# Expert units of 128 rows in place of 256, with the first-layer weights of all experts held on chip

## The chip, the cores and the metric

The kernel runs on one core of a Trainium2 chip. The core has five engines that run side by side and meet at semaphores: TensorE (PE in the rows, with its weight loads as PEld) multiplies, VectorE (DVE) and ScalarE (ACT) work element by element, GpSimd (POOL) issues the indirect DMAs here, and SyncE (SP) issues plain DMAs. Each engine has a sequencer that reads its instructions in order; it executes register loads, waits and branches itself (a q behind the engine's name in the rows) and hands the others to the engine. The metric is the time of one execution on the device in microseconds (us).

## The reference

Two blocks with a residual each: a two-layer graph convolution (mean over neighbours) over 3125 nodes of 256 features and 50,000 edges, and a mixture of 8 experts, of which each node uses 2. Cut to what matters here:

```python
def _moe(tokens, router_w, w1, b1, w2, b2):      # tokens: layernorm(x), 3125 x 256
    probs = softmax(tokens @ router_w.T)          # 8 experts
    rw, re = top_k(probs, 2);  rw = rw / rw.sum(-1, keepdims=True)
    combine = zeros((N, E)).at[arange(N)[:, None], re].set(rw)
    out = tokens
    for e in range(E):
        h = gelu(tokens @ w1[e] + b1[e], approximate=False)
        y = h @ w2[e] + b2[e]
        out = out + combine[:, e:e + 1] * y
    return out
x = x + gnn(layernorm(x), edges, ...)
x = x + _moe(layernorm(x)[None], ...)[0]
```

The 3125 nodes make 6250 pairs of node and expert. On the reference's inputs the experts 0 to 7 get 568, 1013, 238, 1264, 432, 590, 862 and 1283 of them (worked out from the inputs with the reference's router); of the first 1536 nodes come 276, 483, 131, 621, 193, 306, 410 and 652.

## The kernel before

Up to about 454 us TensorE computes the graph convolutions: dense adjacency tiles in SBUF (`adj`, 25 blocks of source nodes) are multiplied with the projected rows, tile by tile of 128 nodes. During the second pass (305 to 454 us) the output of each tile is normed and its two experts are chosen on DVE, and POOL writes each node's row with its routing data (`XW` = 264 numbers: 256 features, two coefficients, two experts, the node's number) to its place in the DRAM table `xs_dram`, which has a region for each expert. From tile 8 on, the part of `adj` that is no longer read takes the second-layer weights and biases of all experts (`ew2_sb`, `eb2_sb`), loaded by SP one expert for each tile.

At the end of the router, each expert's region is padded by `PAIR` rows of zeros (`pad_experts`, 4 DMAs on SP and 4 on ACT), and DVE works out tables with an entry for each unit (L1078 to L1111): its first row (`tab_ri`), its expert (`tab_ei`) and how many units must have landed before its scatter may go out (`tab_wi`). The semaphore `table` tells the others that they are ready. `NTAB` entries (36) stand in each table.

Then comes the expert stage. A unit is `PAIR` = 256 rows of one expert in two halves `h`; the loops run over rounds of `UNITS` = 4 units, here 7 rounds for 28 units. For unit i, buffers go by s = i % 2, the result and id buffers by u = i % 4. Each engine has a fixed order for each unit, written out by hand:

- SP waits until rows of unit i+1 are transposed (`xe_tr`) and their routing data kept (`meta_in`), loads the rows of unit i+3 into `xe` (L470), waits for the hidden layer of unit i (`hid`) and loads the first-layer weights of unit i+2 into `w1_of` (L475). `row_of` (L467) and L474 first load a register from a table.
- PE: `result(i)`, the second layer (L1409; half, then two contraction steps); `hidden(i + 2)`, the first layer (L1398, 4 matmuls with 256 columns, each in two passes); `turn_rows(i + 3)`, 4 transposes (L1389).
- ACT: `weigh(i)`, the sum times the coefficient, one ACTIVATE for each half (L1597); `gelu(i + 2)` (L1588); the copy of the transposed rows (L1582).
- DVE: `result(i)`: loads the expert's number into a register (L1128), waits for `meta_in` and for the landing of the scatter that used the buffer before (`ye_out`), copies the node numbers to `ids` (L1132), waits for `ye_ps`, adds the second-layer bias into `ysum` (L1135). `keep_meta(i + 3)`: waits for the rows, copies the node numbers (L1119), and by a test of the chosen expert sets the coefficient (L1121), once for each half.
- POOL: loads the unit's entry of `tab_wi` into a register (L609), waits for the scatters before it (L612), waits for `ye_in`, and adds the half's 128 rows to `out` in DRAM by an indirect DMA (L616), once for each half.

The order of the work around the change is set by these programs and by the semaphores between them; no scheduler moves anything. A matmul in float32 stands as two instructions, and the profile's count of them is double that of the code.

Of the kernel before, what the change touches and what calls it, by code (L numbers as in the profile page):

```python
# [14 lines left out]
P = 128  # L15
# [4 lines left out]
def build(nc, x, src, dst, w1l, w1r, b1, w2l, w2r, b2, router_w, ew1, eb1, ew2, eb2, out):  # L20
# [41 lines left out]
    PAIR = 2 * P  # L62
# [13 lines left out]
    with ExitStack() as ctx:  # L76
# [174 lines left out]
        assert 2 * NE <= NT and KD == 2  # L251
# [18 lines left out]
        def halves(a):  # L270
            return a.rearrange("p (h n) -> p h n", h=2)

        xe = [halves(expert([2 * XW], F32)) for _ in range(2)]
# [3 lines left out]
        ysum = [halves(expert([2 * D], F32)) for _ in range(2)]  # L277
        ye = [halves(expert([2 * D], F32)) for _ in range(UNITS)]
        xt_ps = [counts_ps[:, s, :] for s in range(2)]
        hid_ps = [counts_ps[:, 2 + s, :] for s in range(2)]  # L280
        y_ps = [halves(bank[2 + s][:, :]) for s in range(2)]
        ids = [expert([2], U32) for _ in range(UNITS)]
        match = [[expert([TOPK], F32) for _ in range(2)] for _ in range(2)]
        tab_c = expert([2 * NTAB], F32)
        tab_id = expert([2 * NTAB], F32)
# [29 lines left out]
                 "ysum_in", "rdeg_in"]  # L315
# [13 lines left out]
        xe_in = [sem(f"xe_in{s}") for s in range(2)]  # L329
        w1_in = [sem(f"w1_in{s}") for s in range(2)]  # L330
# [28 lines left out]
        def pad_experts(engine, of):  # L359

            engine.wait_ge(S["ends"], 1)
            engine.wait_ge(S["zeros"], 1)
            for e in of:
                end = engine.value_load(end_i[0:1, e:e + 1], min_val=e * REGION, max_val=e * REGION + N)
                engine.dma_start(xs_dram[bass.ds(end, PAIR), :].rearrange("(h p) n -> p h n", p=P),
                                 pad_t.rearrange("p (h n) -> p h n", h=1).to_broadcast((P, 2, XW))
                                 ).then_inc(S["padded"], 16)

        @block.sync
        def _(sp):  # L370
# [73 lines left out]
            with sp.Fori(0, NE) as e:  # L444
# [5 lines left out]
                             ).then_inc(S["ew_in"], 16)  # L450
                sp.dma_start(ew(eb2_sb, e, 0), eb2[bass.ds(e, 1), :].to_broadcast((P, D))).then_inc(S["ew_in"], 16)
# [10 lines left out]
            for u in range(UNITS):  # L462
                sp.wait_ge(ye_out[u], 32)
# [5 lines left out]
            def load_rows(row, s):  # L469
                sp.dma_start(xe[s], xs_dram[bass.ds(row, PAIR), :].rearrange("(h p) n -> p h n", p=P)  # L470
                             ).then_inc(xe_in[s], 16)

            def load_w1(i, s):
                e = sp.value_load(tab_ei[0:1, bass.ds(i, 1)], min_val=0, max_val=NE - 1)  # L474
                sp.dma_start(w1_of[s], ew1[bass.ds(e, 1), :, :].rearrange("a (k p) n -> p (a k) n", p=P)  # L475
                             ).then_inc(w1_in[s], 16)
# [6 lines left out]
            load_w1(0, 0)  # L483
            load_rows(row_of(1), 1)
            load_w1(1, 1)
            third_row = row_of(2)
            sp.wait_ge(S["xe_tr"], 1)
            sp.wait_ge(S["meta_in"], 1)
            load_rows(third_row, 0)
            rounds = sp.value_load(nround_i[0:1, 0:1], min_val=MIN_ROUNDS, max_val=MAX_ROUNDS)  # L490

            with sp.Fori(0, rounds) as n:
                for u in range(UNITS):
                    i, s = n * UNITS + u, u % 2
                    row = row_of(i + 3)
                    sp.wait_ge(S["xe_tr"], n * UNITS + (u + 2))
                    sp.sem_inc(S["held"], 1)
                    sp.wait_ge(S["meta_in"], n * UNITS + (u + 2))
                    sp.sem_inc(S["held"], 1)
                    load_rows(row, 1 - s)  # L500
                    sp.wait_ge(S["hid"], n * UNITS + (u + 1))
                    sp.sem_inc(S["held"], 1)
                    load_w1(i + 2, s)

            for u in range(UNITS):
                sp.wait_ge(ye_out[u], rounds * 32 + 32)
# [1129 lines left out]
```

## Time and profile before

| | us |
|---|---|
| median of 3 runs (623.62 to 624.03) | 623.7 |
| span of the profiled execution (its own time in the profile) | 621.3 |
| TensorE busy | 557.1 |
| DVE busy | 351.8 |
| ACT busy | 223.1 |
| POOL busy | 182.1 |
| first load of an expert's rows | 478.19 |
| first and last bias add on DVE (27 steps) | 493.19, 605.21 |
| end of the last scatter-add on POOL | 613.78 |

The profile is of one execution; the span runs from its first to its last instruction, and the run's time holds what lies around it, 2.4 us between the span and the median. Busy shares count the work of an engine and not its register, branch and semaphore instructions. Times on the rows are counted from the start of the span.

### The profile page before, as it was taken

The page shows a single profiled execution, that of the slowest core. Times are in us where ns is not written, and L with a number is a line of the kernel's source. Part 1 is how long each engine was busy: PE and PEld are TensorE (multiplying, and loading weights), DVE is VectorE, ACT ScalarE, POOL GpSimd, SP SyncE. Part 2 cuts the span into 40 slices and gives each one's busy share as a digit, 9 for nine tenths or more (in the row PEclk, how much of TensorE's full clock was granted, in tenths as well). Part 3 has the DMA queues.
Part 4 walks back from the last instruction along what each step waited for, and adds up shares of the span by engine and source line. Part 5 has one row for each costly group of instructions (what it writes and reads, how often), then busy time and mean ns, then how long its engine had stood idle before and what let it go on. Part 6 is the DMA issues. An engine that isn't in the chain of part 4 may idle for free.

```text
span 621.3 us, 11268 instructions
## 1 busy us (share of the span) xinstructions
PE 557.1 (90%) x3021; PEld 331.3 (53%) x3022; DVE 351.8 (57%) x1200; ACT 223.1 (36%) x422; POOL 182.1 (29%) x181
## 2 busy tenths in 40 slices
PE   5999989999999999999999999999930999999991
PEld 3444545555555555554454544544510788887870
DVE  5987656676677667652457576676676133323320
ACT  5666834444444444341001000000000355555551
POOL 4840000000000000000310533534362076667784
PEclk9999999999999999999999999999965799999997
DMA  8421201111110111114621346533326499889992
GB/s 263 134 72 51 89 16 51 52 43 35 52 51 29 50 52 43 34 52 103 205 77 61 121 154 185 170 115 121 97 98 206 133 182 192 165 180 186 178 185 30
DMA packets 70327, 67.01 MB, mean 108 GB/s; under 512 B 11633, under 2 KB 68318, under 8 KB 70286
## 3 DMA queue, kind: packets, MB, share of 16 engines
q1 hardware_dynamic: 53406, 50.61, 27.4%
q0 software_dynamic: 11200, 14.40, 12.2%
q10 hardware_dynamic: 5680, 1.49, 1.1%
q8 instruction: 21, 0.34, 0.2%
q14 instruction: 20, 0.16, 0.1%
HBM read 38.11 MB, written 29.30 MB: 109 GB/s over the span
## 4 chain that ended last, share of the span: by engine, by line
PE 58%; issue 13%; DVE 10%; DMA 7%; POOL 6%; SPq 3%; ACT 1%; POOLq 0%; DVEq 0%; ACTq 0%
PE bank L1256 21%; PE counts_ps L643 6%; PE bank L1246 6%; PE bank L1171 6%; PE counts_ps L1398 6%; DMA adj<-in_L_ffn_w 4%; PE counts_ps L1256 4%; POOL xs_dram L577 3%; PE bank L1409 3%; POOL stat L570 2%; PE counts_ps L1389 2%; DMA y<-y_dram 1%; SPq L474 1%; PE bank L1239 1%; PE bank L1161 1%
## 5 line engine op out<-in xcount | busy, mean ns | idle before, releaser
L1256 PE MATMUL bank<-y,adj 128*128 128x512 f16 x625 | 154.7, 379 | 0.4 <-ACT zt L1464 0.4
L1256 PE MATMUL counts_ps<-y,adj 128*128 128x512 f16 x625 | 144.5, 379 | 1.9 <-DMA y<-y_dram 1.9
L616 POOL DMA_INDIRECT out<-adj x56 | 86.9, 1551 | 52.5 <-ACT adj L1597 27.4
L650 ACT ACTIVATE adj<-counts_ps 128x1000 f32 (+1 forms) x80 | 80.2, 1005 | 61.1 <-PE counts_ps L643 61.1
L1256 PEld LDWEIGHTS counts_ps<-y,adj 128*128 128x128 f16 x625 | 60.6, 101 | 64.7 <-DMA y<-y_dram 3.8
L1256 PEld LDWEIGHTS bank<-y,adj 128*128 128x128 f16 x625 | 57.9, 97 | 59.5 <-issue 13.7
L553 POOL IOTA onehots<- 128x8 int32 x1 | 0.1, 143 | 231.9 <-PE counts_ps L643 231.9
L1398 PE MATMUL counts_ps<-adj 128*128 128x256 f32 x240 | 60.3, 395 | 3.9 <-DMA adj<-in_L_ffn_w 3.6
L1561 ACT ACTIVATE rows<-bank 128x256 f32<-128x256 f32 x25 | 9.6, 383 | 130.3 <-PE bank L1330 119.1
L643 PEld LDWEIGHTS counts_ps<-onehots 125*128 125x128 f16 x640 | 41.0, 98 | 27.1 <-ACT adj L650 10.9
L629 DVE TENSOR_TENSOR onehots<-iota,lo_t 125x1024 f16<-125x1024 f16 x80 | 54.7, 683 | 0.2
L1398 PEld LDWEIGHTS counts_ps<-adj 128*128 128x128 f32 x240 | 45.6, 196 | 15.5 <-issue 8.7
L629 DVE TENSOR_TENSOR onehots<-iota,key_t 125x1000 f16<-125x1000 f16 x80 | 53.8, 673 | 0.0
L643 PE MATMUL counts_ps<-onehots 125*128 125x125 f16 x640 | 51.0, 221 | 2.5 <-DVE onehots L629 2.5
L1409 PE MATMUL bank<-adj 128*128 x224 | 53.0, 379 | 0.0
L1171 PE MATMUL bank<-w,rows 128*128 128x512 f32 x100 | 48.8, 611 | 2.7 <-ACT rows L1449 2.2
L1246 PE MATMUL bank<-w,rows 128*128 128x512 f32 x100 | 47.0, 592 | 0.0
L1135 DVE TENSOR_TENSOR adj<-bank,adj 128x512 f32<-128x512 f32 x28 | 19.4, 692 | 45.2 <-PE bank L1409 41.8
L1597 ACT ACTIVATE adj<-adj 128x256 f32<-128x256 f32 x56 | 25.4, 501 | 49.9 <-DVE adj L1135 41.3
L1409 PEld LDWEIGHTS bank<-adj 128*128 128x128 f32 x224 | 40.5, 190 | 4.4
L1389 PE MATMUL counts_ps<-ident,adj 128*128 128x128 f32 x124 | 20.1, 288 | 16.4 <-DMA adj<-xs_dram 16.4
L909 DVE SCALAR_TENSOR_TENSOR rows<-bank,rdeg,rows 128x256 f32<-128x256 f32 x25 | 12.1, 484 | 39.8 <-PE bank L1256 39.8
(233 smaller groups left out, 621.9 us busy)
## 6 DMA issues: line engine op xcount, KB each, us to landing
adj<-in_L_ffn_w SPq DMA_DIRECT2D x38, 256.0 KB
adj<-xs_dram SPq DMA_DIRECT2D x31, 264.0 KB
rows<-z_dram SPq DMA_DIRECT2D x49, 128.0 KB
z_dram<-zt SPq DMA_DIRECT2D x36, 128.0 KB, 1.7
rows<-in_x SPq DMA_DIRECT2D x24, 128.0 KB
out<-yo SPq DMA_DIRECT2D x24, 128.0 KB
y_dram<-yo SPq DMA_DIRECT2D x23, 128.0 KB, 1.7
y<-y_dram SPq DMA_DIRECT2D x4, 640.0 KB, 6.6
```

The source lines that it names most:

```text
L616: g.indirect_dma_start(out, bass.IndirectOffsetOnAxis(ap=ids[u][:, h:h + 1], axis=0), ye[u][:, h, :], None, bounds_check=N - 1, oob_is_err ...
L629: last = nc.vector.tensor_tensor(oh[0:RUN, slot, :].rearrange("p (g k w) -> p g k w", k=n, w=HALF), iota_4[0:RUN, 0:n, :].rearrange("p (g ...
L643: last = nc.tensor.matmul(counts_ps[:, 2 * slot + bank_of, at * P:at * P + KEYS], stat_g[:, :, h:h + 1].rearrange("p k a -> p (k a)"), mov ...
L650: nc.scalar.activation(adj[:, :, bass.ds(at, GW * WD)].rearrange("p b (h d) -> p b h d", d=WD), counts_ps[:, 2 * (group % 2):2 * (group % ...
L1135: v.tensor_tensor(ysum[s], y_ps[s], ew(eb2_sb, e, 0).rearrange("p (h n) -> p h n", h=1) .to_broadcast((P, 2, D)), ALU.add).then_inc(S["ysu ...
L1171: last = te.matmul(out_of[t % 2][:, :], nrm_t_of[t % 2][:, k * P:(k + 1) * P], w[:, k, :], start=(k == 0), stop=(k == KD - 1))
L1246: last = te.matmul(bank[1][:, :], nrm_t[:, k * P:(k + 1) * P], w[:, k, :], start=(k == 0), stop=(k == KD - 1))
L1256: last = te.matmul(to, adj[:, b, t * P:(t + 1) * P], y[:, b, :], start=(b == 0), stop=(b == NT - 1))
L1389: last = te.transpose(xt_ps[s][:, k * PAIR + h * P:k * PAIR + (h + 1) * P], xe[s][:, h, k * P:(k + 1) * P], ident[:, :])
L1398: last = te.matmul(hid_ps[s][:, m * PAIR:(m + 1) * PAIR], w1_of[s][:, k, m * P:(m + 1) * P], xe_t[s][:, k * PAIR:(k + 1) * PAIR], start=(k ...
L1409: last = te.matmul(y_ps[s][:, h, :], ge_t[s][:, m * PAIR + h * P:m * PAIR + (h + 1) * P], ew(ew2_sb, e, m), start=(m == 0), stop=(m == KD ...
L1597: a.activation(ye[u][:, h, :], ysum[s][:, h, :], ACT.Copy, scale=tab_c[:, bass.ds(i * 2 + h, 1)]).then_inc(S["ye_in"], 1)
```

## The change

`PAIR` becomes 128, so a unit is one block of 128 rows, and there are 52 units in 13 rounds. The halves go, and with them one of the two scatter-adds, weighings, tests and half of the transposes, second-layer matmuls and row loads of a unit; the hidden layer keeps its four matmuls, each with 128 columns. `xe` and `xe_in` get four buffers in place of two, so that the rows of unit i+4 are asked for when those of unit i are transposed. The first-layer weights of all experts are loaded in the second pass with the second-layer ones into `ew1_sb`, the next 8 blocks of `adj`; in the expert stage DVE copies them to `w1_of` (`keep_w1`), where it needs the expert's number in a register. The work on `tab_w` moves behind the flag `table`, with a flag of its own (`before_in`) for POOL. `NTAB` becomes 60.

```diff
-    PAIR = 2 * P
+    PAIR = P
...
+        ew1_sb = adj[:, 2 * NE:3 * NE, 0:2 * KD * D].bitcast(F32)
...
-        xe = [halves(expert([2 * XW], F32)) for _ in range(2)]
+        xe = [expert([XW], F32) for _ in range(UNITS)]
...
             with sp.Fori(0, NE) as e:
...
+                sp.dma_start(ew1_sb[:, bass.ds(e, 1), :].rearrange("p a (k n) -> p (a k) n", n=D),
+                             ew1[bass.ds(e, 1), :, :].rearrange("a (k p) n -> p (a k) n", p=P)
+                             ).then_inc(S["ew_in"], 16)
...
             load_rows(first_row, 0)
-            load_w1(0, 0)
-            load_rows(row_of(1), 1)
-            load_w1(1, 1)
...
+            for u in range(1, UNITS):
+                load_rows(row_of(u), u)
...
                 for u in range(UNITS):
-                    i, s = n * UNITS + u, u % 2
-                    row = row_of(i + 3)
-                    sp.wait_ge(S["xe_tr"], n * UNITS + (u + 2))
+                    row = row_of(n * UNITS + (u + UNITS))
+                    sp.wait_ge(S["xe_tr"], n * UNITS + (u + 1))
...
-                    load_rows(row, 1 - s)
-                    sp.wait_ge(S["hid"], n * UNITS + (u + 1))
-                    sp.sem_inc(S["held"], 1)
-                    load_w1(i + 2, s)
+                    load_rows(row, u)
...
             pool.wait_ge(S["table"], 1)
+            pool.wait_ge(S["before_in"], 1)
...
-                    for h in range(2):
-                        pool.wait_ge(S["ye_in"], n * (2 * UNITS) + (2 * u + h + 5))
...
+                    pool.wait_ge(S["ye_in"], n * UNITS + (u + 3))
...
-            link(v.tensor_tensor(landed, past, over(weight, 2 * NE), ALU.mult))
...
-            dve.wait_ge(S["ew_in"], 16 * 2 * NE)
+            dve.wait_ge(S["ew_in"], 16 * 3 * NE)
...
+            def keep_meta(i, u, arrived):
+                dve.wait_ge(xe_in[u], arrived)
+                v.tensor_copy(tab_id[:, bass.ds(i, 1)], xe[u][:, NODE_ID:NODE_ID + 1])
+                v.scalar_tensor_tensor(match[u], xe[u][:, CHOSEN:NODE_ID], tab_ef[:, bass.ds(i, 1)],
+                                       xe[u][:, COEF:CHOSEN], ALU.is_equal, ALU.mult,
+                                       accum_out=tab_c[:, bass.ds(i, 1)]).then_inc(S["meta_in"], 1)
+
+            def keep_w1(i, s):
+                e = dve.value_load(tab_ei[0:1, bass.ds(i, 1)], min_val=0, max_val=NE - 1)
+                v.tensor_copy(w1_of[s].rearrange("p k n -> p (k n)"),
+                              ew1_sb[:, bass.ds(e, 1), :].rearrange("p a n -> p (a n)")).then_inc(S["w1_in"], 1)
...
+            keep_w1(0, 0)
+            keep_w1(1, 1)
+            link(v.tensor_tensor(landed, past, over(weight, 2 * NE), ALU.mult))
+            link(v.tensor_reduce(tab_w, landed.rearrange("p e j -> p j e"), AX.X, ALU.add))
+            v.tensor_copy(tab_wi, tab_w).then_inc(S["before_in"], 1)
             keep_meta(0, 0, 16)
             keep_meta(1, 1, 16)
-            keep_meta(2, 0, 32)
+            dve.wait_ge(S["hid"], 1)
+            keep_w1(2, 0)
+            keep_meta(2, 2, 16)
+            keep_meta(3, 3, 16)
             with dve.Fori(0, rounds) as n:
                 for u in range(UNITS):
                     result(n * UNITS + u, n, u)
-                    keep_meta(n * UNITS + (u + 3), 1 - u % 2, n * 32 + 16 * ((u + 3) // 2 + 1))
+                    keep_w1(n * UNITS + (u + 3), 1 - u % 2)
+                    keep_meta(n * UNITS + (u + UNITS), u, n * 16 + 32)
...
-                pe.wait_ge(w1_in[s], arrived)
+            def hidden(i, s):
+                pe.wait_ge(S["w1_in"], i + 1)
...
-                    hidden(i + 2, s, n * 32 + 16 * (u // 2 + 2))
-                    turn_rows(1 - s, n * 32 + 16 * ((u + 3) // 2 + 1))
+                    hidden(i + 2, s)
+                    turn_rows(u, n * 16 + 32)
...
-                    turn_rows(i + 3, 1 - s)
+                    turn_rows(i + UNITS, s)
```

What stands on DVE in one unit of the loop before, from the bias add of a unit to the waits ahead of the next unit's copy of the ids (ISA are register steps, some of which wait; TENSOR_LOAD is the load of a register from `tab_ei`):

```order
L1135 TENSOR_TENSOR adj<-bank,adj 128x512
L1118 REGISTER_ALU
L1119 ISA [waits xe_in0]
L1119 COPY adj<-adj 128x2
L1121 ISA
L1121 SCALAR_TENSOR_TENSOR adj<-adj 128x2
L1121 ISA
L1121 SCALAR_TENSOR_TENSOR adj<-adj 128x2
L1128 ISA
L1128 TENSOR_LOAD adj
L1128 ISA x2
L1132 ISA [waits meta_in,ye_out2]
```

The same place on DVE after, from the bias add to the second register load:

```order
L1117 TENSOR_TENSOR adj<-bank,adj 128x256
L1104 ISA
L1104 TENSOR_LOAD adj
L1104 ISA x2
L1105 ISA
L1105 COPY adj<-adj 128x512
L1098 ISA [waits xe_in1]
L1098 COPY adj<-adj 128x1
L1099 ISA
L1099 SCALAR_TENSOR_TENSOR adj<-adj 128x2
L1110 ISA
L1110 TENSOR_LOAD adj
```

and on DVE from there to the next bias add, where before a REGISTER_ALU (L1133) stood ahead of the last wait:

```order
L1110 ISA x2
L1111 REGISTER_ALU
L1114 ISA [waits meta_in,ye_out2]
L1114 COPY adj<-adj 128x1
L1117 ISA [waits ye_ps,ye_in]
L1117 TENSOR_TENSOR adj<-bank,adj 128x256
```

A test has gone, and a second register load with its three register steps, one more step and the copy of 512 numbers have come in between the bias add and the routing data.

SP's loop for one unit before, the load of the weights and that of the rows:

```order
L474 ISA [waits hid]
L474 TENSOR_LOAD adj
L474 ISA x2
L475 ISA
L475 DMA adj<-in_L_ffn_w 128x2x256
L467 ISA
L467 TENSOR_LOAD adj
L467 ISA x2
L496 REGISTER_ALU
L470 ISA [waits xe_tr,meta_in]
L470 DMA adj<-xs_dram 128x2x264
```

and on SP after:

```order
L465 ISA
L465 TENSOR_LOAD adj
L465 ISA x2
L482 REGISTER_ALU
L468 ISA [waits xe_tr,meta_in]
L468 DMA adj<-xs_dram 128x264
```

The weight load and its register load have gone from SP's loop, and the row load no longer stands behind the wait for `hid`.

## Rows read from the trace of the kernel before

**Rows 1.** The page: busy us (share of the span) xinstructions; chain by line; POOL's scatter-adds.

```profile
PE 557.1 (90%) x3021; PEld 331.3 (53%) x3022; DVE 351.8 (57%) x1200; ACT 223.1 (36%) x422; POOL 182.1 (29%) x181
...
PE bank L1256 21%; PE counts_ps L643 6%; PE bank L1246 6%; PE bank L1171 6%; PE counts_ps L1398 6%; DMA adj<-in_L_ffn_w 4%; PE counts_ps L1256 4%; POOL xs_dram L577 3%; PE bank L1409 3%; POOL stat L570 2%; PE counts_ps L1389 2%; DMA y<-y_dram 1%; SPq L474 1%; PE bank L1239 1%; PE bank L1161 1%
...
L616 POOL DMA_INDIRECT out<-adj x56 | 86.9, 1551 | 52.5 <-ACT adj L1597 27.4
```

**Rows 2.** Timeline, one unit: start us, us, engine, line, operation, tiles, count [idle before].

```profile
508.95 1.89 PE L1398 MATMUL counts_ps<-adj 128*128 128x256 f32 x8
...
510.68 0.60 PE L1389 MATMUL counts_ps<-ident,adj 128*128 128x128 f32 x4
...
511.12 1.89 PE L1409 MATMUL bank<-adj 128*128 x8
```

**Rows 3.** Timeline, start of the expert stage.

```profile
478.19 0.41 SPq L470 DMA_DIRECT2D adj<-xs_dram  x1
479.36 0.41 SPq L475 DMA_DIRECT2D adj<-in_L_ffn_w  x1
...
481.73 1.11 PE L1389 MATMUL counts_ps<-ident,adj 128*128 128x128 f32 x4 [15.49 <-DMA adj<-xs_dram]
...
484.70 3.62 PE L1398 MATMUL counts_ps<-adj 128*128 128x256 f32 x8
...
491.06 1.89 PE L1409 MATMUL bank<-adj 128*128 x8
...
493.19 0.69 DVE L1135 TENSOR_TENSOR adj<-bank,adj 128x512 f32<-128x512 f32 x1 [5.49 <-PE bank L1409]
```

**Rows 4.** Timeline, the last bias add.

```profile
605.21 0.69 DVE L1135 TENSOR_TENSOR adj<-bank,adj 128x512 f32<-128x512 f32 x1 [2.59 <-PE bank L1409]
```

**Rows 5.** Timeline of POOL: behind a stall, and the last.

```profile
526.85 1.55 POOL L616 DMA_INDIRECT out<-adj  x1 [3.85 <-issue]
...
612.23 1.55 POOL L616 DMA_INDIRECT out<-adj  x1 [0.30 <-issue]
```

**Rows 6.** Timeline of DVE: bias add to ids, and ids to bias add, without waits.

```profile
529.82 0.69 DVE L1135 TENSOR_TENSOR adj<-bank,adj 128x512 f32<-128x512 f32 x1 [1.95 <-PE bank L1409]
...
531.46 0.17 DVE L1132 CAST adj<-adj 128x2 uint32 x1 [0.60 <-DVE adj L1121]
...
571.48 0.18 DVE L1132 CAST adj<-adj 128x2 uint32 x1 [2.85 <-DMA out<-adj]
571.79 0.69 DVE L1135 TENSOR_TENSOR adj<-bank,adj 128x512 f32<-128x512 f32 x1
```

**Rows 7.** By source line, DVE's sequencer: ns min/median/max, first and last start; then one unit.

```profile
L1128 DVEq TENSOR_LOAD <-adj x28: 301/317/581, 486.4 to 601.5; - x28
...
L1121 DVEq FUSED_REGOPS  x56: 65/82/117, 493.4 to 605.7; - x56
...
L1128 DVEq FUSED_REGOPS  x2: 65/128/190, 530.5 to 530.9; - x2
...
L1131 DVEq EVENT_SEMAPHORE  x1: 50/50/50, 531.2 to 531.2; - x1
```

**Rows 8.** Timeline of DVE across the end of the loop.

```profile
505.24 0.69 DVE L1135 TENSOR_TENSOR adj<-bank,adj 128x512 f32<-128x512 f32 x1 [2.42 <-PE bank L1409]
...
507.50 0.18 DVE L1132 CAST adj<-adj 128x2 uint32 x1 [1.22 <-issue]
```

**Rows 9.** Groups of DVE by form: busy us, mean ns of one.

```profile
L766 DVE CAST adj<-adj 100x500 f32<-100x500 int32 x1 | 0.4, 414 | 0.0
```

**Rows 10.** Windows: us, busy PE, PEld, DVE, ACT, POOL, PEclk, DMA share, GB/s.

```profile
375.00:400.00 25.00, 24.04 (x128) 12.54 (x127) 17.23 (x78) 1.77 (x5) 10.36 (x13) 1.00 0.54 168
...
75.00:85.00 10.00, 7.55 (x53) 4.08 (x52) 6.97 (x13) 3.41 (x5) 0.00 (x0) 1.00 0.27 85
```

**Rows 11.** Timeline: a scatter-add, and a DVE copy that starts beside it.

```profile
509.33 1.55 POOL L616 DMA_INDIRECT out<-adj  x1 [0.30 <-issue]
...
509.96 0.40 DVE L1119 COPY adj<-adj 128x2 f32 x1
```

More of the change, by code:

```diff
@@ L276, in build @@
         ge_t = [expert([KD * PAIR], F32) for _ in range(2)]
[L277 to L285, printed above, removed]
+        ysum = [expert([D], F32) for _ in range(2)]
+        ye = [expert([D], F32) for _ in range(UNITS)]
+        xt_ps = [counts_ps[:, s, 0:KD * PAIR] for s in range(2)]
+        hid_ps = [counts_ps[:, 2 + s, 0:KD * PAIR] for s in range(2)]
+        y_ps = [bank[2 + s][:, 0:D] for s in range(2)]
+        ids = [expert([1], U32) for _ in range(UNITS)]
+        match = [expert([TOPK], F32) for _ in range(UNITS)]
+        tab_c = expert([NTAB], F32)
+        tab_id = expert([NTAB], F32)
         cnt = expert([NE], F32)
@@ L328, in build @@
         scattered = [sem(f"scattered{q}") for q in range(2)]
-        xe_in = [sem(f"xe_in{s}") for s in range(2)]
-        w1_in = [sem(f"w1_in{s}") for s in range(2)]
+        xe_in = [sem(f"xe_in{u}") for u in range(UNITS)]
         ye_out = [sem(f"ye_out{u}") for u in range(UNITS)]
@@ L1382, in _, with turn_rows @@
             prefix(NB - 1)
-            def turn_rows(s, arrived):
-                pe.wait_ge(xe_in[s], arrived)
-                for h in range(2):
-                    for k in range(KD):
-                        last = te.transpose(xt_ps[s][:, k * PAIR + h * P:k * PAIR + (h + 1) * P],
-                                            xe[s][:, h, k * P:(k + 1) * P], ident[:, :])
+            def turn_rows(u, arrived):
+                pe.wait_ge(xe_in[u], arrived)
+                for k in range(KD):
+                    last = te.transpose(xt_ps[u % 2][:, k * P:(k + 1) * P], xe[u][:, k * P:(k + 1) * P], ident[:, :])
                 last.then_inc(S["xe_tr"], 1)
-            def hidden(i, s, arrived):
-                pe.wait_ge(w1_in[s], arrived)
+            def hidden(i, s):
+                pe.wait_ge(S["w1_in"], i + 1)
                 pe.wait_ge(S["xe_t_in"], i + 1)
@@ L1406, in result @@
                 pe.wait_ge(S["ysum_in"], i + 1)
-                for h in range(2):
-                    for m in range(KD):
-                        last = te.matmul(y_ps[s][:, h, :], ge_t[s][:, m * PAIR + h * P:m * PAIR + (h + 1) * P],
-                                         ew(ew2_sb, e, m), start=(m == 0), stop=(m == KD - 1))
+                for m in range(KD):
+                    last = te.matmul(y_ps[s], ge_t[s][:, m * PAIR:(m + 1) * PAIR],
+                                     ew(ew2_sb, e, m), start=(m == 0), stop=(m == KD - 1))
                 last.then_inc(S["ye_ps"], 1)
@@ L1416, in _ @@
             turn_rows(1, 16)
[L1417 to L1420 removed]
+            hidden(0, 0)
+            turn_rows(2, 16)
+            hidden(1, 1)
+            turn_rows(3, 16)
+            pe.wait_ge(S["ew_in"], 16 * 3 * NE)
             pe.sem_inc(S["ysum_in"], 2)
```

79 lines of the change are left out of this document (24 added, 55 removed).

## The prediction

> **What bounds the kernel now.** I read first the table of busy shares, then the stage after 478 us, where the diff works. The busy table alone says TensorE [rows 1]; the views of the expert stage say something finer. The timeline of one unit of 256 rows shows TensorE's pattern, each group's start against the next: 1.73 us of hidden layer, 0.44 of transposes, and a second layer as long as the hidden one, 3.9 us with no hole [rows 2]. The 28 units take 27 steps from the first bias add on DVE at 493.19 to the last at 605.21, so 4.15 a unit: 0.25 more than TensorE needs, and the chain puts 4% of the span (25 us) on the load of the first-layer weights [rows 1, 3, 4]. Behind TensorE stands POOL: 56 scatter-adds of 1.55 us with 0.30 between, 1.86 each, 104 us in 118; most of the rest are three stalls, one of them 3.85, where it has to wait until an earlier expert's rows have landed [rows 1, 5]. At the end POOL alone is late: the last bias add ends at 605.90, the last scatter-add at 613.78, and 7.5 us later the span ends [rows 4, 5]. DVE looks idle. But a busy share counts no register work, and this is what I look at next.
>
> **DVE's sequence, which the busy share hides.** In a unit that waits for nothing, the bias add starts at 529.82 and the copy of the ids, the next step of the loop, at 531.46: 1.64 us [rows 6]. The instructions between them are the copy and the two tests of the routing data and a load of the expert's number into a register: the register rows run from 530.5 to 531.2, so the load costs about 0.74 us with its address and check, though the load itself has a median of 0.317 [rows 7]. From the ids to the next bias add, with nothing to wait for, it takes 0.31 (571.48 to 571.79) [rows 6]. So DVE needs 1.95 a unit of 256 rows, and once in four units 0.6 more for the loop's end (2.26 in place of 1.64) [rows 6, 8]. That is half of 4.15 and costs nothing now.
>
> **Units.** The experts get 568, 1013, 238, 1264, 432, 590, 862 and 1283 rows. Rounded up to 256 that is 28 units in 7 rounds, as the 56 scatter-adds bear out; rounded up to 128 it is 52 units in 13 rounds, with none idle. Work by the row falls by 7%; work by the unit grows by 52/28.
>
> **TensorE after.** Second layer: 4 pairs of load and matmul where 8 took 1.73, 0.87. Transposes: two, 0.22. Hidden layer: still 8 pairs, with 128 columns each. If columns set the time it is 0.87; if the weight load did, more. The nearest row, four transposes of 128 columns in 0.44, has the same shape at 0.11 a pair [rows 2]: the load hides, 0.88. Sum 2.0, with seams 2.05.
>
> **POOL after.** 52 x 1.86 is 97 us. Only one unit (the sixteenth) must wait for the one right before it, three for the second before. At a step above 2 us these stalls fit into POOL's slack, taken as nothing; their upper end is the 4 us of one old stall.
>
> **DVE after, the term that decides.** A unit of half the rows keeps every step of the loop but one test, and gains the copy of the weights with a register load of its own. From 1.95: one test less, 0.2 (its register step of 0.082 [rows 7] and the dispatch); one register step less before the bias add, 0.1; a second register load, 0.74; the issue of the weight copy, 0.16 (a register step as that of a test, 0.082, and a dispatch [rows 7]); a quarter of the loop's end, 0.15. Sum 2.70 a unit. The work of the copy itself (0.42, as a cast of 500 elements took 0.414 [rows 9]) lies behind the next register load and costs nothing on top; without that cover it would be 0.42 x 52, 22 us. Bounds: 2.55 when all steps are at their shortest, 2.85 when the loads average 0.37 (their longest is 0.581). I take 2.70: only the count of steps is new, each step's price is a row. DVE is then later than TensorE (2.05) and POOL (1.86), and everyone waits for it: TensorE for the copied weights and the free result bank, ACT for the sum, POOL for the weighed rows.
>
> The Trainium skill, page "DMA: Bandwidth & Descriptors", section "Latency and other measured facts", gives a register load a floor of about 600 ns; the rows here have a median of 317, so the measurement decides, and by the page two loads would make the step 3.26.
>
> **What is taken away and moved ahead of the loop.** The 28 loads of 256 KB leave SP's queue, and the row loads follow each other one step of SP apart instead of two, 1.17 [rows 3]. The eight weight loads now go out on SP in tiles 8 to 15 of the second pass, at most 1.17 of SP time each, ahead of the next tile's rows; TensorE is busy 24.04 of 25 us there [rows 10] and two tiles ahead of DVE's need, so nothing, at most 1 us. The padding writes halve and the sum of 16 x 36 moves behind the flag "table", but the tables grow from 36 to 60 columns: the flag comes 0.7 earlier. First rows are asked for at 477.0 instead of 478.19.
>
> **The start.** Before: load at 478.19, transposes at 481.73, hidden layer of unit 0 at 484.70 in 3.4 us at half clock, second layer of unit 0 at 491.06, bias add at 493.19 [rows 3]. After: load of unit 1 at 478.2, so its transposes can start at 481.7 as unit 0's did; from 481.8 the first hidden layer and second one take half, 1.7 each, and two more transposes 0.43 each: 483.5, 483.9, 485.6, 486.05; second layer 1.7 at half clock, 487.8; bias add at 488.0. DVE's own work ahead of the loop (two copies, the moved sum, 3 us) is done by 486. Clock: that first hidden layer takes 3.62 where one in the loop takes 1.89 [rows 2, 3], half clock; at 75 to 85 us the granted clock is 1.00 (2.4 GHz) with TensorE busy 7.55 of 10 [rows 10]. A step of 2.7 with 2.0 of work is about that share, so full clock after the start; nothing added.
>
> **The sum.** Last bias add: 488.0 + 51 x 2.70 = 625.7. From there 0.42 of add (an estimate: 0.69 for 512 columns, half of it and a fixed part), 0.17 to ACT, 0.51 + 0.08 to POOL, 1.55 of scatter-add, 7.5 to the end: 10.25. Span 635.9, 14.6 over 621.3. The median is 2.4 over the profiled span, added on both sides: **638.3**. By terms: the start gains 5.2, the end 5.8 (one scatter-add is queued at the end instead of several), the steps cost 25.7 (137.7 for 112.0). The forecast's own range is 626 (2.55, start at 486.5) to 649 (2.85, start at 490).
>
> **Rivals.**
> A. *DVE is not late* (chance 0.09): if register work overlaps more than the rows say, TensorE's 2.05 is the step: 488.0 + 104.6 + 10.25 + 2.4 = 605. For it: DVE has 57% busy and TensorE 90% in the page; the weight loads on the path are gone. Against it: the 1.64 and 0.31 were measured with no wait in them. The side turns at (621.3 - 10.25 - 488.0) / 51 = 2.41 us a unit: the second register load must cost under 0.45.
> B. *POOL becomes the bound* (0.08): copies of DVE and the descriptor work of POOL stand in each other's way. In the trace a DVE copy of two elements takes 0.40, where the copies of the ids take 0.17 and 0.18 [rows 6], when it starts 0.63 after a scatter-add of POOL: and ends when the scatter-add is 1.03 old [rows 11]. A copy of 0.42 in each unit would make POOL's step 1.86 + 0.42 = 2.28: 489.2 + 51 x 2.28 + 1.55 + 7.5 + 2.4 = 617. It decides only if DVE's own step is under 2.28, so if A's condition holds. Under my forecast it costs nothing.
> The rule is that of the Trainium skill, page "SBUF", section "SBUF: two separate sides": an fp32 copy within SBUF locks GpSimd out while it writes descriptors; the row agrees that one waits for the other, here DVE for POOL.
> C. *Register loads slow down* (0.03): at the 0.6 of the longest row, 2 x 0.28 more a unit, 3.26: 667.
> D. *DVE's engine waits for POOL's port in nearly every unit* (0.04): its 1.46 of work (0.17, 0.42, 0.42, 0.16, 0.29) and a whole scatter-add of 1.55 in series give 3.0: 654. Against it: the copy of [rows 11] came through 1.03 after the scatter-add's start, not at its end.
> E. *No change* (0.02): a step near 2.41.
>
> That the change does something else is hardly possible: the loads, copies and 13 rounds follow from the code and the counts; three rows over 1280 in the last expert make its eleventh unit, but 51 units are 13 rounds too.
>
> **How the numbers follow.** Forecast 0.74, A 0.09, B 0.08, C 0.03, D 0.04, E 0.02. The time is the forecast's, 638.3. Slower by over 0.2% (1.2 us, about what a measurement of this kernel can tell from no change): 0.74 + 0.03 + 0.04 = 0.81; within 0.2%: 0.02; faster: 0.17. For 8 in 10 the range takes in B and the forecast: 616 to 651.
>
> **What would show it.** Right: bias adds on DVE 2.6 to 2.8 apart with almost no idle time put down to TensorE, scatter-adds over 2.5 apart, TensorE's busy share of the stage near 75%, the first bias add near 488. Wrong: bias adds 2.1 to 2.3 apart (A or B; in B with gaps of POOL at 0.30 and scatter-adds of 2 us), scatter-adds unchanged but DVE copies of 1 us and more (D), a granted clock of 0.50 beyond 490 us, or a second pass whose last full tile on TensorE ends after 455.

## The result, and the profile after

The changed kernel takes 639.19 us (median; 638.79 to 639.73), the kernel before 623.66 in the same comparison: a ratio of 1.025, 95% interval 1.0236 to 1.0263. It is 2.5% slower. The forecast was 638.3, in a range of 616 to 651.

Of the page of the changed kernel: busy us (share of the span) xinstructions; the first steps of the chain by engine and by line; the scatter-adds.

```profile
PE 563.7 (88%) x3185; PEld 329.4 (52%) x3186; DVE 383.0 (60%) x1316; ACT 233.6 (37%) x491; POOL 174.3 (27%) x173
...
PE 46%; issue 16%; DVE 16%; DVEq 11%; POOL 5%; DMA 3%; ACT 1%; POOLq 0%; SPq 0%; ACTq 0%
PE bank L1246 21%; PE counts_ps L625 6%; PE bank L1236 6%; PE bank L1161 5%; DVEq L1104 4%; PE counts_ps L1246 4%; DVEq L1110 3%; POOL xs_dram L560 3%; POOL stat L553 2%; DMA y<-y_dram 1%; DVE adj L1098 1%; DVE adj L1099 1%; DVEq L1099 1%; PE bank L1229 1%; DMA z_dram<-zt 1%
...
L598 POOL DMA_INDIRECT out<-adj x52 | 80.8, 1554 | 73.1 <-ACT adj L1583 62.4
```

Beside [rows 1] the busy shares tell almost nothing: TensorE 88% for 90%, DVE 60% for 57%. The chain tells it. DVEq, the sequencer of DVE, which no busy share counts, has 11% of it, with the two register loads L1104 and L1110 as its largest lines; the wait for the first-layer weights has gone. POOL has fewer scatter-adds and waits longer, 62.4 of its 73.1 us for ACT, which waits for DVE.

The timeline of the changed kernel, at the start of the expert stage, at the end, and one unit of DVE in between (541.81 to 544.87):

```profile
487.21 0.42 DVE L1117 TENSOR_TENSOR adj<-bank,adj 128x256 f32<-128x256 f32 x1 [1.52 <-PE bank L1396]
...
626.29 0.42 DVE L1117 TENSOR_TENSOR adj<-bank,adj 128x256 f32<-128x256 f32 x1
...
628.24 1.55 POOL L598 DMA_INDIRECT out<-adj  x1 [0.97 <-ACT adj L1583]
```

```profile
541.81 0.15 DVE L1114 CAST adj<-adj 128x1 uint32 x1 [0.99 <-DVE adj L1099]
542.05 0.42 DVE L1117 TENSOR_TENSOR adj<-bank,adj 128x256 f32<-128x256 f32 x1
542.91 0.43 DVE L1105 COPY adj<-adj 128x512 f32 x1 [0.44 <-issue]
543.26 0.15 DVE L1098 COPY adj<-adj 128x1 f32 x1
543.32 0.21 DVE L1099 SCALAR_TENSOR_TENSOR adj<-adj 128x2 f32<-128x2 f32 x1
543.46 0.08 DVE L1099 DVE_READ_ACCUMULATOR adj<-adj  x1
544.64 0.15 DVE L1114 CAST adj<-adj 128x1 uint32 x1 [1.10 <-issue]
544.87 0.42 DVE L1117 TENSOR_TENSOR adj<-bank,adj 128x256 f32<-128x256 f32 x1
```

The 51 steps from the first bias add to the last take 139.08 us, 2.73 each, where [rows 3, 4] gave 27 steps of 4.15. The second fence shows what stands between two bias adds: two holes, 0.44 and 1.10 us, each put down to "issue": the profile shows nothing that the engine waited for, and its sequencer was still at work. The sequencer's rows by source line say at what: ns min/median/max, first and last start.

```profile
L1104 DVEq TENSOR_LOAD <-adj x55: 301/308/435, 477.6 to 626.4; - x55
...
L1110 DVEq TENSOR_LOAD <-adj x52: 300/354/636, 484.5 to 624.9; - x52
```

The load is the register load of the expert's number; an address step of 0.19 and a check stand behind each. The bias add itself waits for TensorE once, in the first unit, as the row of 487.21 says and the view by line sums up (us in all, times):

```profile
  PE bank L1396: 1.5, 1
```

### The profile page after: what moved, and what is told of

Read it like the earlier page. It is cut to its first block, busy times and chain, and to the rows that moved or that the text cites. A ratio compares the mean times of both kernels' runs of the same rounds, so it can differ in the third digit from the quotient of the medians.

```text
span 637.0 us, 12987 instructions
## 1 busy us (share of the span) xinstructions
PE 563.7 (88%) x3185; PEld 329.4 (52%) x3186; DVE 383.0 (60%) x1316; ACT 233.6 (37%) x491; POOL 174.3 (27%) x173
## 4 chain that ended last, share of the span: by engine, by line
PE 46%; issue 16%; DVE 16%; DVEq 11%; POOL 5%; DMA 3%; ACT 1%; POOLq 0%; SPq 0%; ACTq 0%
PE bank L1246 21%; PE counts_ps L625 6%; PE bank L1236 6%; PE bank L1161 5%; DVEq L1104 4%; PE counts_ps L1246 4%; DVEq L1110 3%; POOL xs_dram L560 3%; POOL stat L553 2%; DMA y<-y_dram 1%; DVE adj L1098 1%; DVE adj L1099 1%; DVEq L1099 1%; PE bank L1229 1%; DMA z_dram<-zt 1%
## 5 line engine op out<-in xcount | busy, mean ns | idle before, releaser
L598 POOL DMA_INDIRECT out<-adj x52 | 80.8, 1554 | 73.1 <-ACT adj L1583 62.4
L1386 PE MATMUL counts_ps<-adj 128*128 128x128 f32 x432 | 63.6, 292 | 16.4 <-DVE adj L1105 16.2
L1386 PEld LDWEIGHTS counts_ps<-adj 128*128 128x128 f32 x432 | 54.2, 196 | 35.3 <-DVE adj L1105 35.0
L1396 PE MATMUL bank<-adj 128*128 x208 | 57.1, 397 | 2.3 <-issue 1.0
L1396 PEld LDWEIGHTS bank<-adj 128*128 128x128 f32 x208 | 35.7, 191 | 10.8 <-issue 6.4
L1105 DVE COPY adj<-adj 128x512 f32 x55 | 23.9, 434 | 27.0 <-issue 26.1
L1576 ACT ACTIVATE adj<-counts_ps,onehots 128x128 f32<-128x128 f32 x108 | 33.8, 364 | 16.6 <-issue 13.9
L1114 DVE CAST adj<-adj 128x1 uint32 x52 | 8.0, 154 | 50.0 <-DVE adj L1099 33.3
```

The source lines that it names most:

```text
L598: g.indirect_dma_start(out, bass.IndirectOffsetOnAxis(ap=ids[u], axis=0), ye[u], None, bounds_check=N - 1, oob_is_err=False, compute_op=AL ...
L1386: last = te.matmul(hid_ps[s][:, m * PAIR:(m + 1) * PAIR], w1_of[s][:, k, m * P:(m + 1) * P], xe_t[s][:, k * PAIR:(k + 1) * PAIR], start=(k ...
L1396: last = te.matmul(y_ps[s], ge_t[s][:, m * PAIR:(m + 1) * PAIR], ew(ew2_sb, e, m), start=(m == 0), stop=(m == KD - 1))
L1576: last = a.activation(ge_t[s][:, m * PAIR:(m + 1) * PAIR], hid_ps[s][:, m * PAIR:(m + 1) * PAIR], ACT.Gelu, bias=b1_t[:, m, bass.ds(e, 1)])
```

## The experiments

My theory: DVE's sequencer sets the step of 2.73, instruction by instruction, and TensorE, ACT and POOL wait for it. The rivals: the work of the copy (or its port, shared with POOL) sets it; the sequencer has slack that the prediction did not see. Beside that, two halves of the change had to be told apart: units of 128 rows, and held weights. Each kernel is compared with the kernel before on the same chip (623.9 to 624.5 there); that kernel took 623.66 beside the changed one, so a difference from the changed kernel's 639.19 can be off by up to 0.9 us.

### The copy without its work

```diff
+            def keep_w1_part(i, s):
+                e = dve.value_load(tab_ei[0:1, bass.ds(i, 1)], min_val=0, max_val=NE - 1)
+                v.tensor_copy(w1_of[s].rearrange("p k n -> p (k n)")[:, 0:8],
+                              ew1_sb[:, bass.ds(e, 1), 0:8].rearrange("p a n -> p (a n)")).then_inc(S["w1_in"], 1)
...
-                    keep_w1(n * UNITS + (u + 3), 1 - u % 2)
+                    keep_w1_part(n * UNITS + (u + 3), 1 - u % 2)
```

> The changed kernel, but in the loop DVE copies 8 of the 512 numbers of the first-layer weights (the register load and the instruction stay; the first three units' weights are kept whole, so later units are computed with the weights of earlier experts). My theory: DVE's sequencer sets the step, the copy's 0.43 us of work lies behind the next register load; the step stays 2.73 us and the time 639 (637 to 640). Rival, DVE's engine or the port shared with POOL sets the step: 0.4 us less in each of 51 steps, 618 to 622.

Measured: 639.26 us (638.09 to 640.88), the step 2.725. The copy, by source line:

```profile
L1110 DVE COPY adj<-adj x52: 170/172/226, 487.5 to 626.5; 128x8 f32 x52
```

The copy takes 0.17 in place of 0.43, and nothing of the 0.26 us x 51 = 13 us comes back. So these 0.26 us of its work, and whatever port it holds in them, are wholly covered in this kernel. The rival falls.

### The copy without its register load

```diff
+            def keep_first_w1(s):
+                v.tensor_copy(w1_of[s].rearrange("p k n -> p (k n)"),
+                              ew1_sb[:, 0:1, :].rearrange("p a n -> p (a n)")).then_inc(S["w1_in"], 1)
...
-                    keep_w1(n * UNITS + (u + 3), 1 - u % 2)
+                    keep_first_w1(1 - u % 2)
```

> The changed kernel, but in the loop DVE copies the whole block of expert 0 for every unit, so keep_w1 needs no register load (the results of the other experts are computed with wrong weights); the copy of 512 numbers stays. My theory: the step loses the register load with its address and check, 0.72 us (0.09 + 0.34 + 0.22 + 0.06 from start to next start in the trace), to 2.01; then TensorE's 2.05 and POOL's 1.86 are next, step 2.05 to 2.15, time 639.2 - 51 x 0.63 = 607 (604 to 612). Rival, the copy is what costs: 637 to 639. Rival, POOL is next at 2.28: 616.

Measured: 614.48 us (613.14 to 615.01), 24.7 below the changed kernel and below the kernel before: ratio 0.9836 (0.9816 to 0.9856). A unit in its timeline:

```profile
505.70 0.42 DVE L1121 TENSOR_TENSOR adj<-bank,adj 128x256 f32<-128x256 f32 x1
506.04 0.42 DVE L1109 COPY adj<-adj 128x512 f32<-128x512 f32 x1
506.37 0.15 DVE L1098 COPY adj<-adj 128x1 f32 x1
506.43 0.27 DVE L1099 SCALAR_TENSOR_TENSOR adj<-adj 128x2 f32<-128x2 f32 x1
506.63 0.08 DVE L1099 DVE_READ_ACCUMULATOR adj<-adj  x1
507.57 0.15 DVE L1118 CAST adj<-adj 128x1 uint32 x1 [0.86 <-DVE adj L1099]
507.81 0.42 DVE L1121 TENSOR_TENSOR adj<-bank,adj 128x256 f32<-128x256 f32 x1
```

The hole of 0.44 ahead of the copy is gone and the copy, still of 512 numbers, follows the bias add at once. So the load is the cost and the copy is not. But the time stayed 7.5 us above the 607 that I expected and 2.5 above the end of its range, and the mean step is 2.21, not 2.05 to 2.15. In time the rival of POOL at 2.28 and 616 is nearer. What is next behind DVE is not settled by this run; the last experiments return to it.

### A third register load

```diff
                     keep_w1(n * UNITS + (u + 3), 1 - u % 2)
+                    dve.value_load(tab_ei[0:1, bass.ds(n * UNITS + u, 1)], min_val=0, max_val=NE - 1)
```

> The changed kernel with one more register load of the expert's number on DVE in each unit, behind the weight copy, whose value nobody uses. My theory: 52 x 0.72 us more, 676 (670 to 682). Rival, DVE's sequencer is not what is late (it catches up in slack): under 650.

Measured: 673.16 us (670.33 to 673.72), the step 3.385. That is 34.0 us for 52 loads, 0.65 each, and it comes straight onto the time. The load's own rows:

```profile
L1134 DVEq TENSOR_LOAD <-adj x52: 299/412/609, 486.1 to 658.7; - x52
L1134 DVEq FUSED_REGOPS  x52: 190/190/190, 486.5 to 659.1; - x52
L1134 DVEq SEQ_ASSERT  x52: 23/23/23, 486.7 to 659.3; - x52
```

0.41 + 0.19 + 0.02 with the gaps between them: 0.65, of which the load itself is a little under two thirds.

### The same load where DVE has time

```diff
                 for u in range(UNITS):
                     result(n * UNITS + u, n, u)
+                    dve.value_load(tab_ei[0:1, bass.ds(n * UNITS + u, 1)], min_val=0, max_val=NE - 1)
```

(in the kernel before)

> The kernel before with one more register load of the expert's number on DVE in each of its 28 units, whose value nobody uses. My theory: DVE needs 1.95 of the 4.15 us of a unit there, so 0.66 more is covered: within 0.2% of the kernel before. Rival (a load on DVE's sequencer delays the routing data or the bias add whatever the slack): 28 x 0.66, 18 us more.

Measured: 624.07 against 623.87 us, ratio 1.0006 (0.9993 to 1.0018). The same instructions that cost 0.65 us a unit at a step of 2.73 cost nothing at one of 4.15. The rival of 18 us falls.

### Held weights alone

The kernel before, units of 256 rows:

```diff
+        ew1_sb = adj[:, 2 * NE:3 * NE, 0:2 * KD * D].bitcast(F32)
...
-                    sp.wait_ge(S["hid"], n * UNITS + (u + 1))
-                    sp.sem_inc(S["held"], 1)
-                    load_w1(i + 2, s)
...
+                    keep_w1(n * UNITS + (u + 3), 1 - u % 2)
                     keep_meta(n * UNITS + (u + 3), 1 - u % 2, n * 32 + 16 * ((u + 3) // 2 + 1))
```

> The kernel before with units of 256 rows, and of the change only the first-layer weights held on chip and copied by DVE with a register load of its own. DVE's step becomes 1.95 + 0.9 = 2.85 and stays under 4.15. Theory 1 (POOL is nearly the bound of the kernel before: 56 x 1.86 and three stalls of 4 us fill its 120 us): only the earlier start is gained, 1 to 3 us, 621 to 623. Theory 2 (the step of 4.15 falls to TensorE's 3.9, as the chain's share of the weight load says): 27 x 0.25 = 7 and the start, 614 to 616.

Measured: 619.57 us (618.21 to 621.63), ratio 0.9916 (0.9897 to 0.9935): 4.6 us faster, between the two theories. (Its profiled execution took 621.63, the longest of its four times. It starts the last matmul of the second pass at 456.85, 2.8 later than the kernel before, and asks for the first rows at 481.07, 2.9 later than [rows 3].) Its timeline, two bias adds and the last three scatter-adds:

```profile
529.50 0.69 DVE L1128 TENSOR_TENSOR adj<-bank,adj 128x512 f32<-128x512 f32 x1 [1.21 <-PE bank L1412]
...
533.39 0.69 DVE L1128 TENSOR_TENSOR adj<-bank,adj 128x512 f32<-128x512 f32 x1 [1.22 <-PE bank L1412]
```

```profile
607.17 1.55 POOL L609 DMA_INDIRECT out<-adj  x1 [0.30 <-issue]
609.02 1.55 POOL L609 DMA_INDIRECT out<-adj  x1 [0.30 <-issue]
610.87 1.55 POOL L609 DMA_INDIRECT out<-adj  x1 [0.30 <-issue]
```

Most steps are 3.89 us now, TensorE's own, and DVE waits for TensorE in most units; the mean is 4.00 for 4.15. But the last bias add is at 602.30 and the last scatter-add starts 8.6 later, where it was 7.0 in the kernel before, and the last scatter-adds follow each other at POOL's 1.85: part of what TensorE gains is queued up in POOL. The weights held on chip are a gain by themselves, here and, as the next run says, for the smaller units too.

### Small units alone

The changed kernel, with the first-layer weights loaded by SP for each unit as before:

```diff
                     load_rows(row, u)
+                    sp.wait_ge(S["hid"], n * UNITS + (u + 1))
+                    sp.sem_inc(S["held"], 1)
+                    load_w1(n * UNITS + (u + 2), u % 2)
...
-                    keep_w1(n * UNITS + (u + 3), 1 - u % 2)
```

> The other part alone: units of 128 rows with four row and result buffers, but the first-layer weights come by DMA from SP for each unit, as before, and DVE has neither the copy nor the second register load. DVE's step is 2.73 - 0.88 = 1.85. Theory 1 (POOL's own step of 2.2, as with the fixed expert, or SP's two issues of 1.17 are next): 2.2 to 2.4 a unit, 614 to 626. Theory 2 (a load of 256 KB each 2.3 us, asked for when the unit two before is through the hidden layer and 3.1 us on its way, is later than that): 2.7 or more, 639 or more.

Measured: 654.7 us (652.8 to 655.6), ratio 1.0487 (1.0457 to 1.0517), step 2.99. Theory 2. Two weight loads on SP, the row load between them, and the hidden layers of that time:

```profile
561.30 0.40 SPq L470 DMA_DIRECT2D adj<-in_L_ffn_w  x1
561.75 1.15 PE L1385 MATMUL counts_ps<-adj 128*128 128x128 f32 x8 [0.73 <-DMA adj<-in_L_ffn_w]
...
563.19 0.35 SPq L466 DMA_DIRECT2D adj<-xs_dram  x1
...
564.45 0.40 SPq L470 DMA_DIRECT2D adj<-in_L_ffn_w  x1
...
565.27 0.93 PE L1385 MATMUL counts_ps<-adj 128*128 128x128 f32 x6 [0.94 <-DMA adj<-in_L_ffn_w]
...
568.17 1.15 PE L1385 MATMUL counts_ps<-adj 128*128 128x128 f32 x8 [0.36 <-DMA adj<-in_L_ffn_w]
```

It is a loop of two units. The hidden layer of 561.75 must end before its weight buffer can be filled again; SP, which has a row load and a register load ahead of it, issues that at 564.45; the page gives the load 3.0 us to land in the median, and the hidden layer two units on starts at 568.17, 3.7 behind the issue. That is 6.4 us for these two units. Over the stage it is 3.4 in the median from the issue to the hidden layer and 2.4 from there to the next issue, and two units take 5.9. That this loop sets the pace is read from these rows; a third weight buffer, which would loosen it, was not tried. The 2.3 us that my expectation gives a load is shown by no row; the DMA engines are 0.81 busy, so they are not full either. So the small units alone cost 30 us, the held weights alone gain 4.6, and both together cost 15.5: in small units the held weights are worth 15 us. What is left of the loss is smaller than the register load that they need on DVE, by the run without it.

### One register load a unit, all computed

```diff
+        b2_of = [expert([D], F32) for _ in range(UNITS)]
...
-            def keep_w1(i, s):
+            def keep_w1(i, s, u):
                 e = dve.value_load(tab_ei[0:1, bass.ds(i, 1)], min_val=0, max_val=NE - 1)
+                v.tensor_copy(b2_of[u], ew(eb2_sb, e, 0))
...
-                e = dve.value_load(tab_ei[0:1, bass.ds(i, 1)], min_val=0, max_val=NE - 1)
...
-                v.tensor_tensor(ysum[s], y_ps[s], ew(eb2_sb, e, 0), ALU.add).then_inc(S["ysum_in"], 1)
+                v.tensor_tensor(ysum[s], y_ps[s], b2_of[u], ALU.add).then_inc(S["ysum_in"], 1)
...
+                    dve.wait_ge(S["ysum_in"], n * UNITS + (u + 2))
```

> The changed kernel computing all of it, with one register load a unit on DVE: the step that copies the first-layer weights of unit i+3 also copies the second-layer bias of that unit to one of four small buffers (256 numbers), so the bias add needs no register. It adds one copy (0.16 of sequencer time) and one wait (0.09), and takes away a load (0.72). Theory 1 (each sequencer step counts, load or not): 2.73 - 0.72 + 0.25 = 2.26, 615 (612 to 619), faster than both kernels but the one with the fixed expert. Theory 2 (the copy's work counts too, now that two copies follow each other behind one load: 0.26 more): 2.5, 628.

Measured: 614.05 us (612.77 to 614.54), ratio 0.9834 (0.9808 to 0.9861), step 2.22: 25 us below the changed kernel, 10.5 below the kernel before. Theory 1. DVE has one copy more than the changed kernel (256 numbers, 0.29 us of work) and one load less, and the load is what counts.

### What is next behind DVE

Three runs on the step of 2.2. First a register load more on POOL, in the kernel with the fixed expert:

```diff
                     before_it = pool.value_load(tab_wi[0:1, bass.ds(i, 1)], min_val=0, max_val=MAX_PAIRS)
+                    pool.value_load(tab_wi[0:1, bass.ds(i, 1)], min_val=0, max_val=MAX_PAIRS)
```

> The fixed-expert kernel (wrong weights for other experts, no register load for the weights) with one more register load on POOL in each unit. Theory 1 (there POOL's sequencer sets the step of 2.21: one register load for each scatter-add where there was one for two): 0.65 more in each of 51 steps, 643 to 649. Theory 2 (POOL's scatter-adds and their landing set it, the sequencer has room under 1.55): 614 to 618.

Measured: 635.19 us (634.06 to 635.26), 20.7 more, 0.40 a unit: between the theories. The load is 0.29 with 0.15 of address step and a check, less than the 0.65 that I had put in. The added load costs 0.40 a unit of the 0.46 of its three rows: POOL's sequencer is close to the step there, and has a little room.

Then one step less on DVE, in the kernel with one register load:

```diff
                 dve.wait_ge(ye_out[u], n * 16 + 16)
-                dve.sem_inc(S["held"], 1)
```

> The kernel with one register load on DVE a unit, without the semaphore step behind the two waits ahead of the copy of the ids (0.09 less on DVE's sequencer). If DVE still sets the step: 4 to 5 us less than the kernel with that step; if POOL does: the same within 1 us.

Measured: 612.69 us (612.20 to 614.34) against 614.05 (612.77 to 614.54), ratio to the kernel before 0.9819 (0.9789 to 0.9848). The difference of 1.4 us is inside the spread of the two, and neither of my two cases fits it well; the 4 to 5 us of a DVE that is late in every unit did not come.

Then POOL's register loads cut to one for four units, on top of that:

```diff
+            link(v.scalar_tensor_tensor(wp[0], by_unit[:, :, 1:2], 64.0, by_unit[:, :, 0:1], ALU.mult, ALU.add))
...
             with pool.Fori(0, rounds) as n:
+                packed = pool.value_load(tab_wi[0:1, bass.ds(n, 1)], min_val=0, max_val=64 ** UNITS - 1)
                 for u in range(UNITS):
-                    i = n * UNITS + u
-                    before_it = pool.value_load(tab_wi[0:1, bass.ds(i, 1)], min_val=0, max_val=MAX_PAIRS)
+                    before_it = packed // 64 ** u % 64
```

> The kernel with one register load on DVE and without the semaphore step, and on POOL one register load for each round of four units: the four counts that the units must wait for stand in one number, taken apart by register arithmetic (DVE packs them ahead of the loop). Theory 1 (POOL's sequencer sets the 2.2 us a unit): a load with its check, 0.65, is replaced by two register steps of 0.1; the step falls to what DVE (about 2.1) or TensorE (2.05) allow, 604 to 609. Theory 2 (the 2.2 are scatter-adds of 1.85 and waits until earlier scatters have landed, 3.8 us behind their start): 611 to 614, no change.

Measured: 612.34 us (612.10 to 613.35), ratio 0.9812 (0.9795 to 0.9830): no change. So with this much taken off POOL's sequencer the step stays: its register loads were not it either. POOL's timeline there:

```profile
519.12 1.55 POOL L600 DMA_INDIRECT out<-adj  x1 [0.30 <-issue]
522.46 1.81 POOL L600 DMA_INDIRECT out<-adj  x1 [1.78 <-DMA out<-adj]
527.76 1.55 POOL L600 DMA_INDIRECT out<-adj  x1 [3.49 <-ACT adj L1590]
530.21 1.55 POOL L600 DMA_INDIRECT out<-adj  x1 [0.91 <-issue]
532.07 1.56 POOL L600 DMA_INDIRECT out<-adj  x1 [0.31 <-issue]
533.93 1.55 POOL L600 DMA_INDIRECT out<-adj  x1 [0.30 <-DMA out<-adj]
```

Around the fifteenth and sixteenth unit, behind an expert with only two units, a scatter-add has to wait until the units of the expert before have landed: steps of 3.34 and 5.30. Behind such a stall POOL works at its 1.85 to 2.0 until it has caught up, and only then do the others set the pace again. There are three such steps in this run (the third is 3.67). Over a pace of 2.0 they are 6.3 us, but POOL makes most of that up: its twelve steps ahead of the first stall have a mean of 2.24, the next 28, with all three stalls in them, 2.21, and the last eleven 2.16. So the stalls do not explain the 2.21. What lifts it above 2.0 stands in the steps of 2.5 to 2.8 that come once a round of four, before and long after the stalls. Which engine's end of the loop makes those was not tried, so that part stays open.

The row of 527.76 names ACT with 3.49 us, but ACT had done its part before that. The timeline of ACT:

```profile
524.53 0.51 ACT L1590 ACTIVATE adj<-adj 128x256 f32<-128x256 f32 x1 [1.06 <-DVE adj L1118]
```

It ends at 525.04. What the scatter-add waits for longer is the landing of the one before, of 522.46: these land 3.8 us after their start in the median by the trace, so near 526.3, and POOL starts again 1.5 us later. That it was this landing is inferred from these times. The name in a row of several waits is the last by the profile, and here it misleads.

## Why the prediction was right

**The bound.** DVE's sequence was read from two gaps of the kernel before, 1.64 and 0.31 us, in units in which nothing waited. That it would be the bound is what the chain, the two "issue" holes and five runs show: a load less takes 25 us away (in two runs), a load more adds 34, the copy's work is worth nothing, and a load in the kernel before is worth nothing.

**The step.** 2.70 forecast, 2.73 measured. Inside a round the steps have a mean of 2.63 and the fourth 3.05. So the loop's end costs 0.42 once in four units, 0.11 a unit for the 0.15 that I took, and the rest 2.63 for the 2.55 of the other terms. The register load was put at 0.74 with its address and check; the run with a third one measured 0.65. So the load and the loop's end were put 0.13 too high, and the smaller terms together (a test and a register step less, the issue of the copy) must be 0.16 too low; no row here splits them further. That the step came out within 0.03 is in part luck; that DVE's sequencer sets it is not. The range has a slip: 486.5 + 51 x 2.55 + 10.25 + 2.4 is 629, not 626.

**The cover of the copy.** Put at nothing, and at 22 us without its cover; the run with 8 numbers in place of 512 gave 639.26 for 639.19. Nothing is right, for the 0.26 us that the run took away; the copy's remaining 0.17 was not taken away by itself.

**The start and the end.** First rows asked for at 477.0 forecast, 477.69 measured; first bias add 488.0 forecast, 487.21 measured; from the last bias add to the end 10.25 forecast, 637.04 - 626.29 = 10.75 measured. The end holds one miss in its parts: from the last bias add to the scatter-add it is 1.95 us, where I had 0.42 + 0.17 + 0.51 + 0.08 = 1.18: the weighing on ACT ends at 627.36, and the scatter-add starts 0.88 behind it in place of 0.08. The rest is 0.25 shorter than thought. In the whole sum, start -0.8, steps +1.4, end +0.5 and the 2.4 between span and median, which is 2.2 here, leave 0.9.

**The second pass.** The eight weight loads were put at nothing, at most 1 us. The last matmul of the pass starts at 455.13, in the kernel before at 454.05, 1.1 later; of this, 0.5 us are there when the pass starts (302.37 for 301.88), and the rest is one longer wait for DVE. The two waits and the two last matmuls, each of after and then of before:

```profile
410.71 0.19 PE L1338 MATMUL bank<-onehots 128*128 128x32 f16 x1 [1.64 <-DVE onehots L1005]
...
455.13 0.38 PE L1246 MATMUL counts_ps<-y,adj 128*128 128x512 f16 x1
```

```profile
409.61 0.19 PE L1348 MATMUL bank<-onehots 128*128 128x32 f16 x1 [0.96 <-DVE onehots L1023]
...
454.05 0.38 PE L1256 MATMUL counts_ps<-y,adj 128*128 128x512 f16 x1
```

So the loads do not come for nothing: in the nine profiled kernels that hold the first-layer weights this matmul starts between 454.37 and 457.17, in the three that do not between 454.05 and 454.12. By what way the loads delay DVE was not tried. In the changed kernel it is some 0.6 us, inside the bound, though the last matmul stands behind the 455 us that the prediction's sign of being wrong names.

**POOL's stalls.** Put at nothing under a step of 2.7, and they are: the changed kernel's POOL has one step of 4.74 us and makes it up in the next four, 2.0 to 2.4.

**Rivals A and B.** A had TensorE's 2.05 as the step and 605 us if DVE is not late. The four kernels in which DVE has one register load a unit and POOL no added one show steps of 2.20 to 2.22 and 612.3 to 614.5 us: 7 to 9.5 us of that rival were not to be had. B, copies of DVE against POOL's port, gave a time in that region, 617, by a POOL step of 2.28. Where DVE is the bound the copy's size changes nothing. Where POOL is near it, in the kernel with packed counts, two scatter-adds and DVE's two copies between them stand so:

```profile
543.65 1.55 POOL L600 DMA_INDIRECT out<-adj  x1 [0.30 <-DMA out<-adj]
...
545.50 1.55 POOL L600 DMA_INDIRECT out<-adj  x1 [0.30 <-DMA out<-adj]
```

```profile
543.73 0.29 DVE L1107 COPY adj<-adj 128x256 f32 x1 [0.54 <-DVE adj L1118]
543.94 0.42 DVE L1108 COPY adj<-adj 128x512 f32 x1
```

POOL keeps 1.55 and its step of 1.85 although both copies run beside the scatter-add, so B's 0.42 on every step is not there. Single ones do stretch: in this run the longest copy of 512 numbers takes 0.75 for a median of 0.42, the longest scatter-add 1.81 for 1.55. The copy's size was not changed in a kernel with this step, so a smaller share of B in the 2.21 stays open.

**Rivals C, D and E.** The register loads did not slow down (medians 0.308 and 0.354, the longest 0.636); DVE's weight copies kept a median of 0.43, with the longest 0.73; D's steps of 3 us in every unit did not come, and E's 2.41 is below the mean at each of the four places in a round (2.56 at the least).

**A sign that was wrong.** I expected TensorE's busy share of the stage near 75%, 2.05 of 2.73. The view of windows gives:

```profile
490.00:620.00 130.00, 111.87 (x665) 85.80 (x664) 57.79 (x287) 66.86 (x190) 73.91 (x48) 1.00 0.60 96
```

That is 86%. The unit's groups of matmuls are recorded at 1.16, 0.38 and 1.03 us; added up that is 2.57, and 2.35 a unit where they overlap (111.87 us over 47.7 units), while back to back I had them advance by 2.05. A group's modelled end lies later than the start of the next one can. So the busy share of an engine with gaps between short groups is too high, and would have hidden that TensorE waits. The granted clock was 1.00 over the stretch, as forecast, with those gaps.

## What to carry to other kernels

When units shrink, ask what each engine pays per unit and not per row: register loads, address steps, checks, waits and loop ends stay as they are, and no busy share counts them. Read an engine's floor per unit from a unit in which it waits for nothing, by the starts of its instructions, and price an added dynamic index at a register load with its address step, about 0.65 us on DVE here. Load an index once and use it for all that hangs on it, or copy what depends on it to a fixed place in the same step: here that turned 2.5% slower into 1.7% faster.

## What the runs showed of the hardware

- A register load with its address step and check costs 0.65 us on DVE's sequencer (34.0 us for 52), though its own median is 0.41 or less; on POOL the same three rows are 0.29, 0.15 and 0.02. In the kernel before, where DVE needs 1.95 of a unit's 4.15 us, it costs nothing that shows (ratio 1.0006).
- Of the work of a DVE copy of 0.43 us that stands between two register loads, 0.26 was free: cut to 0.17 it changed 639.19 to 639.26, far inside the spread.
- DVE copies of 0.29 and 0.42 us beside a scatter-add of POOL left it at 1.55 us and its step at 1.85 (543.65 us of the run with packed counts); the longest of that run was 1.81.
- Weights fetched by DMA for each unit into two buffers go with a slower pace: 3.4 us from the issue to the matmuls that use them and 2.4 from there to the next issue, and 5.9 for two units (all medians; 2.99 a unit in the mean). The DMA engines were less busy than in the kernel before, 0.81 of 495 to 620 us against 0.89 of 495 to 600.
